# A two-layer transformer kernel: the order of the mixing layer, with gating moved on GpSimd and normalisation in pairs of tiles

## The chip, the cores and the metric

The kernel runs on one core of one Trainium2 chip. The metric is the device time of one execution in microseconds, the median of several runs. A core has five engines that run their own instruction lists in order and meet only at semaphores: TensorE (PE), VectorE (DVE), ScalarE (ACT), GpSimd (POOL) and SyncE (SP, which here issues transfers).

## The reference

The input is x, 2048 tokens of 256 numbers. Two layers follow one another, each with an attention-like part and a mixture of experts, both gated and modulated. The change touches only the first part of the second layer, the mixing layer:

```python
h = _layernorm(x, axis=-1) * (1 + ca) + sa          # outer normalisation, modulated
x = x + ga * _L1_attn_ref(h, ...)                   # ga: a vector of 256
# _L1_attn_ref(X, ...), X of 2048 rows:
Xn = _layernorm(X, gamma, beta)                     # nested normalisation
Q, K, V = jnp.split(Xn @ W_in + b_in, 3, axis=-1)
K, V = _rotary(K, 128), _rotary(V, 128)
A = jnp.sum(_cos_sim(K) * _cos_sim(V), axis=-2)
Y = (0.5 * A + 0.5)[:, None, :] * Q
return Y @ W_out + b_out + X                        # X is h, so x also gets ga * h
```

In the kernel the token axis is one sequence of 2048, as the input has batch 1.

## The kernel before

The tokens lie as 16 tiles of 128 (`NT = 16`), handled in quarters of four (`TQ = 4`, `NC = 4`). The mixing layer is `phase_mix` (line 1614). Each engine has its own block in it, with the order of its steps written out by hand.

Step by step for a quarter q, with the code's names:

- `stats(q)` (VectorE, `ln_stats`, lines 73 to 83) takes mean and variance of x; `outer(q)` on GpSimd (`ln_rstd`, line 103) raises the variance to the power -1/2; `outer_bias(q)` (VectorE, line 124) makes the bias; `outer(q)` on ScalarE (`ln_normal`, line 132) writes the normalised rows into `k.h`; `modulate(q)` (VectorE, lines 141 and 142) multiplies and adds.
- The same follows for the nested normalisation, from `k.h` into `xn`: `nested_stats(q)`, `nested(q)` on GpSimd, `nested_bias(q)`, `nested(q)` on ScalarE.
- `turn(q)` on TensorE transposes `xn` (line 150) into two PSUM banks `tp`, and `turned(q)` on ScalarE (line 1882) copies them to `xnT` with gamma and beta.

And for each tile i:

- `keys_values(i)` (TensorE, lines 1956 and 1958): first values, then keys, each in one of two PSUM banks. Keys of tile i wait until VectorE has finished tile i - 2.
- `products(i)` (VectorE): copies the values to SBUF (line 1780), waits for the first of the two `squares(i)` (ScalarE, line 1894, which give the norms), and makes the two products (lines 1783 and 1786).
- `turn_products(i)` (GpSimd, line 1712) multiplies by the rotation.
- After four tiles `token_weights(q)` (GpSimd, lines 1718 and 1722) makes the weights, and `sum_products(q)` (TensorE, line 1968) sums the quarter into `pA`.

Behind the last tile TensorE transposes expert weights of the next part (`turn_weights`, line 902), VectorE makes `A_rows` (lines 1830 to 1839), TensorE and VectorE make `A`, `w_sc` (1844), `w_c` (1846) and `b_all` (1848), and then the residual loop adds, tile by tile, the product `xnT` by `w_c` (TensorE, line 2024, two PSUM banks) to `k.x` (VectorE, line 1857) and takes the statistics for the router. At the head of each quarter VectorE adds `b_all` (line 1854). This needs `add_gated(q)` of GpSimd (lines 1726 and 1729): `k.h` times the gate `ga`, added to `k.x`.

The orders that matter here:

- GpSimd: the powers, then the rotations of all 16 tiles with `token_weights(q)` after each fourth, then `add_gated` of all four quarters.
- VectorE: `products(0)` to `products(3)` alternate with `nested_stats(2)`, `modulate(3)` and `nested_stats(3)`; `products(4)` to `products(15)` follow without normalisation between them.
- TensorE: `turn(q + 1)` stands behind `keys_values(4q + 1)`.
- ScalarE: ten weight copies (`keep_half`), `outer(0)` to `outer(2)`, two more copies, and later `nested(q + 2)` inside quarter q.
- SyncE: a weight load (`load_raw(4)`) waits for the last rotation; the weight transposes behind `A` need it.

## Time and profile before

| | |
|---|---|
| median of 3 runs | 1109.9 us (1108.56 to 1111.27) |
| the profiled execution, its own time | 1106.7 us |
| its span on the core | 1104.8 us, 24791 instructions |
| TensorE busy | 972.3 us (88%) |
| VectorE busy | 640.9 us (58%) |
| ScalarE busy | 521.5 us (47%) |
| GpSimd busy | 300.9 us (27%) |
| mixing layer | about 718 to 821 us of the span |

The profile shows one execution. A time in a row is the start in microseconds from the start of the span, followed by the duration. A bracket behind a row says how long the engine had been idle before it and who released it. The shares of the whole span say little on the mixing layer, which is a tenth of it: there the engines alternate, and the rows are read stage by stage.

### The profile page before, as it was taken

The numbers are of one execution on the slowest core, as the hardware profiler recorded it, in microseconds if no ns is written. First come the engines' busy times: TensorE is split into PE (matmuls) and PEld (weight loads), VectorE is DVE, ScalarE is ACT, GpSimd is POOL, SyncE is SP. The second block draws the span as 40 slices with busy tenths as digits, with TensorE's granted clock in tenths as the row PEclk, the third lists the DMA queues.
The fourth block names the chain that finished last, engine by engine and source line by source line (L and its number), as shares of the span: only waits on it lengthen the run. The fifth ranks groups of instructions, "written<-read, shape, count | busy, mean of one in ns | idle before, by whom it ended". The sixth has DMA issues, their size and how long they took to land. (4 is left out here: it accounts for less than half of the span.)

```text
span 1104.8 us, 24791 instructions
## 1 busy us (share of the span) xinstructions
PE 972.3 (88%) x9939; PEld 636.8 (58%) x9943; DVE 640.9 (58%) x1643; ACT 521.5 (47%) x813; POOL 300.9 (27%) x347
## 2 busy tenths in 40 slices
PE   7789899999999999886499999859857699999993
PEld 4334334445444444343277777647644699999993
DVE  5578999999799888754600000187586633333331
ACT  4434567777865875755121221276325233333330
POOL 2100510011011111230233432235830245554541
PEclk9888999999999999998699999969888799999997
DMA  5880000000000000007833785121324023222224
GB/s 187 181 170 4 2 2 3 2 3 3 2 3 2 3 3 3 3 2 251 261 113 102 203 251 166 20 77 58 119 66 141 24 46 50 47 47 48 47 43 96
DMA packets 63275, 78.81 MB, mean 71 GB/s; under 512 B 12096, under 2 KB 54976, under 8 KB 62736
## 3 DMA queue, kind: packets, MB, share of 16 engines
q1 hardware_dynamic: 50688, 61.54, 18.5%
q0 software_dynamic: 11968, 15.47, 8.8%
q8 instruction: 65, 1.06, 0.4%
q10 hardware_dynamic: 528, 0.52, 0.1%
q14 instruction: 26, 0.21, 0.1%
HBM read 58.12 MB, written 21.36 MB: 72 GB/s over the span
## 5 line engine op out<-in xcount | busy, mean ns | idle before, releaser
L594 ACT ACTIVATE k_prob<-f_s 128x1024 f32<-128x1024 f32 (+3 forms) x320 | 269.9, 896 | 119.2 <-PE f_s L432 118.6
L654 DVE TENSOR_REDUCE k_mpart<-f_r 128x1 f32<-128x512 f32 x384 | 250.6, 685 | 34.1 <-PE f_r L375 31.8
L375 PE MATMUL f_r<-k_ks,k_qs 112*32 112x512 bf16 (+3 forms) x2560 | 211.4, 356 | 19.6 <-DVE k_mpart L654 7.8
L432 PE MATMUL f_s<-k_qs,k_ks 114*32 114x512 bf16 (+3 forms) x2560 | 174.2, 349 | 1.9 <-ACT k_prob L594 1.3
L850 POOL TENSOR_SCALAR_AFFINE_SELECT k_prob<-k_prob 128x256 f32<-128x256 f32 x128 | 51.2, 406 | 380.8 <-ACT k_prob L594 379.6
L375 PEld LDWEIGHTS f_r<-k_ks,k_qs 112*32 112x32 bf16 x2560 | 70.0, 95 | 135.2 <-DVE k_mpart L654 55.9
L448 PE MATMUL f_o<-k_prob,k_vaug 128*32 128x512 f32 (+3 forms) x1280 | 146.0, 528 | 1.5 <-POOL k_prob L850 1.4
L651 DVE CUSTOM_DVE_ANT_0 k_unread<-f_r,k_causal 128x128 bf16<-128x128 f32 (+3 forms) x256 | 121.2, 484 | 17.2 <-PE f_r L375 16.0
L432 PEld LDWEIGHTS f_s<-k_qs,k_ks 114*32 114x32 bf16 x2560 | 65.5, 97 | 78.0 <-issue 27.1
L2192 DVE TENSOR_TENSOR mid<-silu_g,e_u 128x512 f32<-128x512 f32 x39 | 26.8, 688 | 111.3 <-PE e_u L2094 110.3
L1348 DVE SCALAR_TENSOR_TENSOR outr<-p_o,k_w,k_mod 128x256 f32<-128x256 f32 x16 | 7.7, 484 | 134.0 <-PE p_o L1283 134.0
L1319 ACT ACTIVATE mid<-p_h 128x320 f32<-128x320 f32 x64 | 28.0, 437 | 111.6 <-PE p_h L1272 111.6
L2094 PEld LDWEIGHTS e_g<-xT,k_rot_t 128*128 128x128 f32 x624 | 76.9, 195 | 4.5 <-ACT xT L2152 2.6
L2280 POOL DMA_INDIRECT sum<-y,k_row_of x39 | 62.1, 1593 | 63.7 <-DVE y L2203 52.7
L2094 PE MATMUL e_g<-xT,k_rot_t 128*128 128x128 f32 x624 | 77.6, 278 | 2.0 <-ACT xT L2152 2.0
L1272 PE MATMUL p_h<-rowsT,k_w1T 128*128 128x320 f32 x256 | 72.6, 442 | 6.5 <-issue 5.5
L2094 PE MATMUL e_u<-xT,k_rot_t 128*128 128x128 f32 x624 | 76.0, 275 | 0.0
L2105 PE MATMUL e_y<-k_w1T,mid 128*128 x312 | 73.6, 379 | 0.0
L2094 PEld LDWEIGHTS e_u<-xT,k_rot_t 128*128 128x128 f32 x624 | 72.8, 192 | 0.0
L912 POOL DMA_INDIRECT k_xb<-h_rows,k_tok_of x39 | 45.3, 1162 | 99.0 <-PE e_x L2088 53.5
L1272 PEld LDWEIGHTS p_h<-rowsT,k_w1T 128*128 128x128 f32 x256 | 48.9, 194 | 28.0 <-issue 9.5
L1366 POOL DMA_INDIRECT sum<-outr,k_row x24 | 37.8, 1576 | 98.1 <-DVE outr L1348 98.1
(388 smaller groups left out, 1288.3 us busy)
## 6 DMA issues: line engine op xcount, KB each, us to landing
k_w1T<-in_L_ffn_w_dram SPq DMA_DIRECT2D x18, 512.0 KB, 10.5
k_w1T<-in_L_ffn_wi_dram SPq DMA_DIRECT2D x8, 1024.0 KB
k_w1T<-in_L_ffn_wo_dram SPq DMA_DIRECT2D x8, 1024.0 KB
k_qs<-q_dram SPq DMA_DIRECT2D x6, 768.0 KB, 9.5
h_rows<-k_h SPq DMA_DIRECT2D x8, 512.0 KB, 4.8
sum<-k_x SPq DMA_DIRECT2D x8, 512.0 KB, 6.5
q_dram<-k_room SPq DMA_DIRECT2D x12, 256.0 KB, 9.3
k_rot_t<-in_L_ffn_w_dram SPq DMA_DIRECT2D x6, 512.0 KB, 4.8
```

The source lines that it names most:

```text
L375: last = nc.tensor.matmul(dst[32 * j:32 * (j + 1), :], qs[0:KROWS, c, GH * g + hs, q0:q0 + 32], ks[0:KROWS, QC * ck:QC * ck + w], start=Tr ...
L432: last = nc.tensor.matmul(sc[h % 2][32 * j:32 * (j + 1), i, off:QC], ks[0:KALL, k0:k0 + 32], qs[0:KALL, c, GH * g + 2 * pair + i, off:QC], ...
L448: last = nc.tensor.matmul(ot[32 * j:32 * (j + 1), off:QC], vaug[:, kt, :], prob[:, u % 2, j, off:QC], start=(kt == 0), stop=(kt == TQ * (c ...
L594: nc.scalar.activation(prob[:, u % 2, 2 * pair:2 * pair + 2, off:QC], sc[h % 2][:, :, off:QC], ACT.Exp, scale=HD ** -0.5).then_inc(e_done, 1)
L651: nc.vector.tensor_tensor_reduce(unread[:, r % RING, 0:w], bank(r)[:, 0:w], causal[:, QC - w:QC], 1.0, NEG, ALU.add, ALU.max, mpart[:, s % ...
L654: nc.vector.reduce_max(mpart[:, s % 2, hs, t, ck:ck + 1], bank(r)[:, 0:w], AX.X).then_inc(ring_used[r % RING], 1)
L850: nc.gpsimd.affine_select(out=block_, in_=block_, compare_op=ALU.is_ge, fill=0.0, base=0, pattern=[[0, 2], [1, P]], channel_multiplier=-1) ...
L912: nc.gpsimd.indirect_dma_start(out=k.xb[:, b % 2, :], out_offset=None, in_=k.h_rows, in_offset=bass.IndirectOffsetOnAxis(ap=k.tok_of[:, b: ...
L1272: last = nc.tensor.matmul(ph[n % 2][:, 0:CAP], wi[:, s, t, P * n:P * (n + 1)], rowsT[:, s, t, :], start=(t == 0), stop=(t == KH - 1))
L2094: last = nc.tensor.matmul(out[:, P * c:P * (c + 1)], w[:, s, F1 * t + P * c:F1 * t + P * (c + 1)], xT[:, s, t, :], start=(t == 0), stop=(t ...
L2105: last = nc.tensor.matmul(py[s][:, :], m[:, s, P * c:P * (c + 1)], k.w1T[:, e, 2, D * c:D * (c + 1)], start=(c == 0), stop=(c == FT - 1))
L2280: nc.gpsimd.indirect_dma_start(out=k.sum1, out_offset=bass.IndirectOffsetOnAxis(ap=k.row_of[:, b:b + 1], axis=0), in_=y[:, s, :], in_offse ...
```

## The change

Nothing is computed otherwise. The quarter is replaced by six spans in the two normalisations and the transposes: four pairs (tiles 0 and 1, 2 and 3, 4 and 5, 6 and 7) and two quarters (8 to 11, 12 to 15). The steps `span_stats`, `span_rstd`, `span_bias` and `span_normal` are the old ones over a span. A pair's four transposes go to one PSUM bank (`tp[g % 2]`) and are copied by two ScalarE instructions of 256 columns.

GpSimd's `add_gated(0)` to `add_gated(2)` stand between its rotations. The gating of the last quarter goes to VectorE, behind `products(15)`. Three of the four additions of `b_all` go from VectorE to GpSimd (`add_bias`). All engines get new orders:

```diff
+SPANS = [(0, 2), (2, 4), (4, 6), (6, 8), (8, 12), (12, 16)]
+PAIRED = 4
...
@@ block.gpsimd
             outer(0)
             outer(1)
             outer(2)
             nested(0)
+            nested(1)
             outer(3)
-            nested(1)
+            nested(2)
             pool.wait_ge(weights_in, 16 * MIX_LOADS)
             pool.wait_ge(tok_zero, 1)
+            outer(4)
             turn_products(0)
-            nested(2)
-            turn_products(1)
-            turn_products(2)
             nested(3)
-            for i in range(3, NT):
+            for i in range(1, 5):
                 turn_products(i)
-                if i % TQ == TQ - 1:
-                    token_weights(i // TQ)
-            for q in range(NC):
-                add_gated(q)
-            for q in range(NC):
+            token_weights(0)
+            add_gated(0)
+            nested(4)
+            outer(5)
+            for i in range(5, 10):
+                turn_products(i)
+            token_weights(1)
+            nested(5)
+            add_gated(1)
+            turn_products(10)
+            turn_products(11)
+            token_weights(2)
+            add_gated(2)
+            for i in range(12, NT):
+                turn_products(i)
+            token_weights(3)
+
+            def add_bias(q):
+                if q == NC - 1:
+                    pool.wait_ge(last_gated, 1)
+                nc.gpsimd.tensor_tensor(quarter(k.x, q), quarter(k.x, q), bcast(b_all[:, :], TQ),
+                                        ALU.add).then_inc(sum_ready, 1)
+
+            pool.wait_ge(wc_ready, 2)
+            for q in range(1, NC - 1):
+                add_bias(q)
+            ln_rstd(nc, pool, k, 0, var3_ready, rstd3_ready)
+            add_bias(NC - 1)
+            for q in range(1, NC):
                 ln_rstd(nc, pool, k, q, var3_ready, rstd3_ready)
...
@@ block.vector
             modulate(0)
             outer_bias(2)
             nested_stats(0)
-            stats(3)
+            modulate(1)
             nested_bias(0)
-            modulate(1)
-            outer_bias(3)
             nested_stats(1)
             modulate(2)
             nested_bias(1)
+            stats(3)
+            nested_stats(2)
+            outer_bias(3)
             products(0)
-            nested_stats(2)
+            nested_bias(2)
             products(1)
+            stats(4)
             modulate(3)
-            nested_bias(2)
+            nested_stats(3)
             products(2)
-            nested_stats(3)
+            nested_bias(3)
             products(3)
-            nested_bias(3)
-            for i in range(TQ, NT):
+            outer_bias(4)
+            products(4)
+            modulate(4)
+            products(5)
+            nested_stats(4)
+            stats(5)
+            nested_bias(4)
+            products(6)
+            outer_bias(5)
+            products(7)
+            products(8)
+            modulate(5)
+            products(9)
+            nested_stats(5)
+            nested_bias(5)
+            products(10)
+            products(11)
...
+            for i in range(12, NT):
                 products(i)
...
+            last = NC - 1
+            dve.wait_ge(normal_h, len(SPANS))
+            step(tt(quarter(k.h, last), quarter(k.h, last), bcast(gate, TQ), ALU.mult))
+            tt(quarter(k.x, last), quarter(k.x, last), quarter(k.h, last), ALU.add).then_inc(last_gated, 1)
             dve.wait_ge(A_done, 1)
...
                 if i % TQ == 0:
                     q = i // TQ
-                    dve.wait_ge(hb_ready, q + 1)
-                    tt(quarter(k.x, q), quarter(k.x, q), bcast(b_all[:, :], TQ), ALU.add).then_inc(sum_ready, 1)
-                    dve.wait_ge(sum_ready, q + 1)
+                    if q == 0:
+                        dve.wait_ge(hb_ready, 1)
+                        step(tt(quarter(k.x, 0), quarter(k.x, 0), bcast(b_all[:, :], TQ), ALU.add))
+                    else:
+                        dve.wait_ge(sum_ready, q)
...
@@ block.scalar
-            for n in range(IN_TAIL, AT_START - 2):
+            for n in range(IN_TAIL, 20):
                 keep_half(n)
             outer(0)
             outer(1)
             outer(2)
...
+            squares(3)
+            turned(3)
+            outer(4)
+            squares(4)
+            squares(5)
+            nested(4)
+            squares(6)
+            turned(4)
+            squares(7)
+            outer(5)
+            squares(8)
+            squares(9)
+            nested(5)
+            squares(10)
+            turned(5)
+            squares(11)
...
@@ block.tensor
-            for q in range(NC):
-                keys_values(TQ * q)
-                keys_values(TQ * q + 1)
-                if q + 1 < NC:
-                    turn(q + 1)
-                keys_values(TQ * q + 2)
-                if q >= 2:
-                    sum_products(q - 2)
-                keys_values(TQ * q + 3)
+            turns = {0: 1, 2: 2, 4: 3, 6: 4, 9: 5}
+            for i in range(NT):
+                keys_values(i)
+                if i in turns:
+                    turn(turns[i])
+                if i in (10, 14):
+                    sum_products(i // TQ - 2)
             sum_products(NC - 2)
             sum_products(NC - 1).then_inc(A_done, 1)
```

ScalarE's order ahead of `squares(3)`, left out above, is: `outer(0)` to `outer(2)`, `keep_half(20)`, `keep_half(21)`, `nested(0)`, `keep_half(22)`, `keep_half(23)`, `turned(0)`, `nested(1)`, `turned(1)`, `squares(0)`, `outer(3)`, `nested(2)`, `squares(1)`, `turned(2)`, `squares(2)`, `nested(3)`. In the names of the new orders the number of a normalisation, turn or bias step is that of a span, and the number of a product, square or rotation that of a tile.

## Rows read from the trace of the kernel before

**Rows 1.** Two stages: length, then each engine's busy time (instructions), granted clock.

```profile
737.00:757.00 20.00, 17.07 (x77) 13.20 (x78) 17.02 (x50) 13.64 (x37) 8.81 (x9) 0.80 0.00 0
757.00:782.00 25.00, 24.57 (x141) 17.53 (x139) 12.89 (x38) 14.36 (x54) 13.15 (x18) 1.00 0.21 64
```

**Rows 2.** Timeline of PE: start, duration, line, output and inputs, idle before.

```profile
737.69 1.94 PE L150 MATMUL m_tp<-k_ident,k_w1T 128*128 128x128 f32 x8 [10.08 <-ACT k_w1T L132]
740.58 0.37 PE L1956 MATMUL m_v<-m_b_part,m_share 128*128 128x256 bf16 x1 [0.96 <-ACT m_xnT L1882]
...
779.43 0.27 PE L1956 MATMUL m_k<-m_b_part,m_share 128*128 128x256 bf16 x1
...
784.58 1.06 PE L1968 MATMUL m_pA<-k_w1T,m_w_tok 128*32 128x512 f32 x8 [3.02 <-issue]
...
788.65 1.44 PE L902 MATMUL m_v<-k_ident,k_w1T 128*128 128x128 f32 x8
791.70 0.60 PE L2002 MATMUL m_tp<-m_ones,m_A_rows 128*128 128x1 f32 x4 [1.61 <-DVE m_A_rows L1839]
```

**Rows 3.** Timelines of PE, ACT and DVE: one tile's keys, square and product.

```profile
776.38 0.27 PE L1956 MATMUL m_k<-m_b_part,m_share 128*128 128x256 bf16 x1
...
777.55 0.38 ACT L1894 ACTIVATE m_sq<-m_k 128x256 f32<-128x256 f32 x1 [1.08 <-PE m_k L1958]
...
778.13 0.42 DVE L1783 TENSOR_TENSOR k_w1T<-m_k,m_vals 128x256 f32<-128x256 f32 x1 [0.99 <-ACT m_sq L1894]
```

**Rows 4.** Timelines of DVE, POOL and ACT: the steps of a quarter's normalisations.

```profile
721.92 1.41 DVE L77 BATCH_NORM_STATS2 k_stats<-k_x 128x6 f32<-128x256 f32 x4 [0.95 <-DMA k_x<-sum]
...
723.86 1.40 DVE L77 BATCH_NORM_STATS2 k_stats<-k_x 128x6 f32<-128x256 f32 x4
...
739.79 1.22 DVE L141 TENSOR_TENSOR k_h<-k_h,k_mod 128x1024 f32<-128x1024 f32 x1
...
742.18 0.16 DVE L124 SCALAR_TENSOR_TENSOR m_nbias<-m_mv,m_rstd 128x4 f32<-128x4 f32 x1
...
747.83 1.01 POOL L103 TENSOR_TENSOR m_rstd<-m_var,k_mhalf 128x4 f32<-128x4 f32 x1 [1.11 <-DVE m_var L82]
...
782.56 1.64 POOL L1718 TENSOR_TENSOR m_inv_n<-m_norm,k_mhalf 128x8 f32<-128x8 f32 x1
...
726.79 4.15 ACT L132 ACTIVATE k_h<-k_x,k_nbias,k_rstd 128x256 f32<-128x256 f32 x8
...
758.13 1.43 ACT L1882 ACTIVATE m_xnT<-m_tp,k_beta,k_gamma 128x512 f32<-128x512 f32 x2
```

**Rows 5.** Timelines of DVE and POOL, where both are at work.

```profile
786.36 0.22 DVE L1833 TENSOR_TENSOR m_A_sum<-m_A_sum,m_pA 128x64 f32<-128x64 f32 x1
...
786.87 2.38 POOL L1729 TENSOR_TENSOR k_x<-k_x,k_h 128x1024 f32<-128x1024 f32 x1
787.08 2.26 DVE L1838 TENSOR_TENSOR m_A_rows<-m_A_sum,m_A_dif 128x64 f32<-128x64 f32 x1
...
748.81 1.64 POOL L1712 TENSOR_TENSOR k_w1T<-k_w1T,k_rot_t 128x256 f32<-128x256 f32 x1
...
802.15 2.35 POOL L1729 TENSOR_TENSOR k_x<-k_x,k_h 128x1024 f32<-128x1024 f32 x1
802.87 0.42 DVE L1857 TENSOR_TENSOR k_x<-k_x,m_k 128x256 f32<-128x256 f32 x1
```

**Rows 6.** Line 884 between 780 and 785 us: the load's issue and its landing.

```profile
L884 SPq DMA_DIRECT2D k_rot_t<-in_L_ffn_w_dram x1: 507/507/507, 783.6 to 783.6; - x1
...
DMA to landing us min/median/max: 5.7/5.7/5.7
```

**Rows 7.** Timeline of PE: first and last matmuls of the residual loop.

```profile
799.22 5.34 PE L2024 MATMUL m_k<-m_w_c,m_xnT 128*128 128x256 f32 x24
...
817.05 1.13 PE L2024 MATMUL m_k<-m_w_c,m_xnT 128*128 128x256 f32 x4
```

**Rows 8.** A stage as in the first group, that follows the 3.02 us of idle PE.

```profile
786.00:789.00 3.00, 3.00 (x17) 3.00 (x15) 2.90 (x6) 1.87 (x4) 2.92 (x2) 0.51 1.07 371
```

More of the change, by code:

```diff
@@ L1611, in _, with span_of, span_stats, span_rstd @@
             gather_row1(nc, k, 0)
+SPANS = [(0, 2), (2, 4), (4, 6), (6, 8), (8, 12), (12, 16)]
+PAIRED = 4
+def span_of(i):
+    return next(g for g, (lo, hi) in enumerate(SPANS) if lo <= i < hi)
+def span_stats(nc, step, k, g, var_ready):
+    tiles = range(*SPANS[g])
+    for i in tiles:
+        last = nc.vector.bn_stats(k.stats[:, i, :], k.x[:, i, :])
+    step(last)
+    for i in tiles:
+        last = nc.vector.bn_aggr(k.mv[:, i, :], k.stats[:, i, :])
+    step(last)
+    s = slice(*SPANS[g])
+    nc.vector.tensor_scalar_add(k.var[:, s], k.mv[:, s, 1], EPS).then_inc(var_ready, 1)
+def span_rstd(nc, pool, k, g, var_ready, rstd_ready):
+    pool.wait_ge(var_ready, g + 1)
+    s = slice(*SPANS[g])
+    nc.gpsimd.tensor_tensor(k.rstd[:, s], k.var[:, s], k.mhalf[:, s], ALU.pow).then_inc(rstd_ready, 1)
+def span_bias(nc, dve, k, g, rstd_ready, bias_ready):
+    dve.wait_ge(rstd_ready, g + 1)
+    s = slice(*SPANS[g])
+    nc.vector.scalar_tensor_tensor(k.nbias[:, s], k.mv[:, s, 0], -1.0, k.rstd[:, s],
+                                   ALU.mult, ALU.mult).then_inc(bias_ready, 1)
+def span_normal(nc, act, k, g, bias_ready, norm_ready):
+    act.wait_ge(bias_ready, g + 1)
+    for i in range(*SPANS[g]):
+        last = nc.scalar.activation(k.h[:, i, :], k.x[:, i, :], ACT.Identity, bias=k.nbias[:, i:i + 1],
+                                    scale=k.rstd[:, i:i + 1])
+    last.then_inc(norm_ready, 1)
 def phase_mix(nc, k, a, sem):
@@ L1904, in _ @@
             outer(2)
-            for n in range(AT_START - 2, AT_START):
-                keep_half(n)
+            keep_half(20)
+            keep_half(21)
             nested(0)
+            keep_half(22)
+            keep_half(23)
             turned(0)
+            nested(1)
+            turned(1)
+            squares(0)
             outer(3)
-            nested(1)
-            for q in range(NC):
-                squares(TQ * q)
-                squares(TQ * q + 1)
-                if q + 1 < NC:
-                    turned(q + 1)
-                squares(TQ * q + 2)
-                if q + 2 < NC:
-                    nested(q + 2)
-                squares(TQ * q + 3)
+            nested(2)
+            squares(1)
+            turned(2)
+            squares(2)
+            nested(3)
+            squares(3)
[14 more added lines that the diff above has]
+            squares(11)
+            squares(12)
+            squares(13)
+            squares(14)
+            squares(15)
             for n in range(AT_START, IN_SUMS):
```

69 lines of the change are left out of this document (42 added, 27 removed).

## The prediction

> **What bounds the kernel now.** I read the stage table first, then the engines' timelines of the mixing layer. No engine bounds this layer throughout [rows 1]. Until about 757 us VectorE is the busy one (17.0 of 20 us); from there to 782 TensorE is busy 24.6 of 25 us. Each is held only where the orders of the engines meet, so I follow those. The reader is to see four places [rows 2]. TensorE waits 10.1 us for the first normalised quarter; `keys_values(0)` starts at 740.6. The last `sum_products` starts at 784.58, after the waits behind the last tile (its `k` product starts at 779.43, [rows 2]). `A_rows` comes only at 791.64, and PE had been free since 790.1. One tile at full clock is a `v` and a `k` product of 0.98 each; from the start of `k` to the square on ScalarE it is 1.17, to VectorE's product 1.75 [rows 3].
>
> **Prices of the parts** [rows 4]. A quarter's statistics take VectorE 1.94 (721.92 to 723.86, the next one's start), its modulation 2.39 (739.79 to 742.18), its normalisation on ScalarE 1.97 (eight tiles in 4.15, 0.49 each), `turned` 1.43. The power on GpSimd takes 1.01 for 4 columns and 1.64 for 8. No pair is in this trace. Estimates from halves plus the fixed part: statistics 1.15 (0.97 to 1.3), modulation 1.35 (1.2 to 1.5), normalisation 1.1, power 0.7 (0.5 to 1.0), `turned` 0.8 to 0.95. `products(i)` holds VectorE 1.0.
>
> **Earlier start.** ScalarE does eight weight copies ahead of `outer(0)`, no longer ten, so is free at 725.5, not 726.8. Then: normalisation 726.55, `modulate(0)` 727.9, nested statistics 729.2, power (it finds `modulate(1)` on VectorE and waits) 730.5, `nested(0)` 731.85, four transposes at half clock 732.95, `turned(0)` 733.9. `keys_values(0)` starts at 734.0: 6.6 us earlier than 740.6.
>
> **What the new orders do to that.** Here the in-order queues decide. Before, the later three quarters are normalised well ahead of PE's turns, which is why PE is busy 24.6 of 25 us there [rows 1]. After, four links are tight.
> - Tiles 0 to 3: `squares(0)` stands behind `turned(1)`, so behind PE's `turn(1)`; `products(0)` ends at 740.6, `products(1)` at 743.3. `products(2)` stands behind `stats(4)` 1.94, `modulate(3)` 1.35, `nested_stats(3)` 1.15; with its own copy (0.45) that is 748.3. `keys_values(4)` needs that copy and PE is free at 744.9: 3.5 us idle. `nested(3)` then lets `turn(3)` start at 750.5 (750.0 to 751).
> - `turn(3)` to `turn(4)`: transposes and signal 0.85, `turned(3)` 0.8, `outer(4)` 1.95, first half of `squares(4)` 0.6, end of `products(4)` 0.55, `modulate(4)` 2.4, `products(5)` 1.0, `nested_stats(4)` 1.95, `stats(5)` 1.95, bias 0.15, `nested(4)` 2.1: 14.3. To it come 0.7, the rotation of tile 4 that takes the port between the two modulation instructions (as in [rows 5] at 748.81), and 1.6, because GpSimd's `nested(4)` now stands behind `token_weights(0)` (1.9) and `add_gated(0)` (4.7) and its power is ready at 765.1 where VectorE is at 763.6. Sum 16.6 (14.1 to 17.5), so `turn(4)` is at 767.1. PE's own work in it (a turn, two tiles, some half clock) is 5 to 6 us. The rest is idle.
> - `turn(4)` to `turn(5)`: `turn(4)` 0.87 to 1.75, `v` of tile 7 0.98 to 1.9, `k` to ScalarE 1.17, `squares(7)` 0.8, `outer(5)` 1.95, first half of `squares(8)` 0.6, end of `products(8)` 0.55, `modulate(5)` with its port wait 3.1, `products(9)` 1.0, `nested_stats(5)` 2.05, GpSimd's power 1.0 behind `turn_products(9)` and `token_weights(1)` (0.65), bias 0.15, `nested(5)` 2.1: 16.2 to 18.7; with the clock half at first, I take 18.2: 785.3. PE waits in it after `keys_values(9)`, about 10 us.
> - `turn(5)` to the `k` of tile 15: 0.87, five tiles 9.75, one `v` 0.98, two `sum_products` 1.94 = 13.5 (to 15.5 at half clock first). I take 15.0: 800.3.
> So the last `k` starts 20.9 us later than 779.43. Lower bound 750.0 + 14.1 + 15.6 + 13.5 = 793.2 (+13.8), upper 751 + 17.5 + 19 + 15.5 = 803 (+23.6).
>
> **Behind the last tile.** Before, `sum_products(3)` starts 5.15 after that `k`. GpSimd now has `add_gated(2)` (4.7) just ahead of the last four rotations, and VectorE has its two gating instructions (1.2 each, two SBUF operands) in the same microseconds as the last rotation and power: they take turns at the port. I count 8.2 (6.2 to 8.5): +3.0 (+1.0 to +3.3).
>
> **What is gained.** GpSimd gates nothing while `A` is made. The first of the two 64-column instructions took 2.26, to the end of GpSimd's addition (786.87 + 2.38), where such a one takes 0.22 (the port again, [rows 5]); the second went the same way, and PE got `A_rows` at 791.7. It will be ready 4.3 us earlier. But PE is then late: it has weight transposes until 790.1, so only the 1.61 counts that PE waited [rows 2] (0.6 if they all run at half clock). The first `w_sc` instruction loses its port wait too, which hides behind PE's next three weight transposes. The weight load that these need was issued at 783.6, behind GpSimd's last rotation, and landed after 5.7, at 789.3 [rows 6]; it moves with that rotation, and PE asks 14 us after the last `k`, the load is there 13 us after it: hidden by 1 us. The residual loop runs on PE from 799.22 to 818.18, 19.0 us [rows 7]; PE waits in it for VectorE, which has a bias addition for each quarter. With three of the four on GpSimd (2.36 each, ready before their tiles: 802.2 and 804.6 on the old axis) it is PE's own 16 x 0.87 + 0.2 = 14.1, less 0.3 for the quarters' ends: a gain of 4.6 (3.3 to 5.1; the low end if `sum_ready` is late once).
>
> **Sum.** +20.9 + 3.0 - 1.6 - 4.6 = **+17.7 us**; bounds +13.8 + 1.0 - 1.6 - 5.1 = +8.1 and +23.6 + 3.3 - 0.6 - 3.3 = +23.0. The profiled execution took 1106.7 (span 1104.8, 1.9 around it), 3.2 below the median. Made against it the sum gives 1124.4; the median moves alike, 1109.9 + 17.7 = 1127.6, and goes on record. Bounds 1118 and 1133.
>
> **Two places where rows and the skill meet.** While GpSimd's gating ran (802.15, 2.35) VectorE's addition with one PSUM operand took 0.42 as ever, while one with two SBUF operands waited to GpSimd's end [rows 5]. The Trainium skill (SBUF — State Buffer, "SBUF: two separate sides") has the same: an exclusive lock, only for a VectorE instruction with two SBUF inputs or in a two-port mode. By the rows `products` runs freely beside `add_gated`; were it locked too, six gating instructions of 2.4 could each hold one up, 14 us more.
> After 3.02 us with PE idle [rows 2] the granted clock is 0.51 from 786 to 789, the 1.2 GHz level [rows 8]. The Trainium skill (TensorE: Matmul & The Clock Gate, "HAM oscillation — how this bites in real kernels") warns that idle gaps between bursts bring the slow clock back each time. It speaks against this change: every one of its waits restarts slow. By the rows one restart costs about 1.5 us (3 us at half rate); all three together are 4.5 of my +20.9.
>
> **The rivals.**
> - The bare order (20%). The links hold, but the soft terms don't: no port waits, `add_gated(0)` over before anyone asks, the clock up again at once. That is the lower bound with some slack, 1113 to 1120, likeliest 1118. For it: pair prices are estimates and ScalarE has room. Against it: GpSimd's order has 6.6 us fixed ahead of `nested(4)`.
> - Faster (9%): the early start is kept. If VectorE's work interleaved without waits, PE would run 38 us from 734 and end about 7 us earlier: -6.6 + 3.0 - 1.6 - 4.6 = -9.8, 1100. For it: VectorE's work of the layer (45 us) fits under PE's. It decides where `nested(4)` ends before `keys_values(6)`, at about 757. Against: VectorE alone, without one wait, has by the prices above 29.5 us of steps ahead of that bias, 721.9 + 29.5 = 751.4, and my walk puts 12 us of waits into them.
> - The parts cancel (4%): 1108 to 1112.
> - Worse than forecast (9%), the other way: gating's 2.4 us holds also small VectorE steps (variance, bias), or GpSimd wins the port against the first bias addition and delays the residual loop by 2.4. 1133 to 1138.
> - Forecast 58%: 1120 to 1133.
>
> **How the numbers follow.** The range 1113 to 1133 holds the forecast and the bare order, 0.78, and the rest of it a little. A measurement of this kernel can tell about 0.2% (2.2 us) from no change. Faster 0.09, same 0.04, slower 0.87. Cases of one sign hold most of it.
>
> **What would show it.** In the profile after: first `keys_values` near 734; then PE idle of 3 to 4 us before tile 4, of some 10 us before `turn(4)` and again before `turn(5)`, both released by ScalarE's normalisation; granted clock near 0.5 behind each; the last `sum_products` 22 to 25 us later; the two `A_rows` instructions at 0.22; residual quarters of 3.5 us. The forecast is wrong if `turn(4)` or `turn(5)` start without a long wait, or if GpSimd's powers never stand behind gating.

## The result, and the profile after

The changed kernel takes **1128.6 us** (median of 4 runs, 1128.32 to 1128.77), the kernel before beside it 1109.6 (4 runs, 1108.56 to 1111.27): a ratio of 1.0162, with a 95% interval of 1.0146 to 1.0178. It is 19.0 us slower; 17.7 had been forecast, 1127.6 in 1113 to 1133. The profiled execution of after took 1128.6 (span 1126.7), that of before 1106.7 (span 1104.8). So the two traces differ by 21.9 us and the medians by 19.0, because the profiled execution of before lay 2.9 below its median.

Where the 21.9 us lie is read by cutting both traces at the same two instructions: the first PE transpose of the mixing layer's `w_in`, and the first transpose of the router behind it. The layer takes 108.73 us before and 130.26 after, 21.53 more. The time ahead of the layer is 1.48 shorter, the time behind it 1.85 longer, and the change touches neither. In the profiled executions of the twelve kernels the layer starts between 716.7 and 722.5 us, and what follows it takes 276.9 to 279.9. The median of the kernel before was taken four times beside the others and lay between 1108.7 and 1111.6. So a difference of a few microseconds between two medians may have nothing to do with an edit inside the layer. I compare whole kernels by their ratios and edits by the length of the layer and its steps. These lengths come from one profiled execution of each kernel. How well they repeat is seen where an edit touches only what comes later: the last `k` stands at 87.23 in after and at 86.98 in `after_tail`. Where the clock differed by chance the difference is 1.7 us, as told at `norm_early`.

The page of after first, in 40 slices of 28.2 us: busy tenths of PE, then the granted clock.

```profile
span 1126.7 us, 24812 instructions
...
PE   7789999999999999968599999663777599999993
...
PEclk9989999999999999997799999886897799999997
```

The slice from 760.5 to 788.7 us has a 3 for PE and a 6 for the clock. That is the stretch where before PE was busy 24.6 of 25 us [rows 1]. The stage table of after (columns as in [rows 1]) has the same two stages, then four of 3 to 4 us: behind the waits for the fifth and sixth span, behind the last wait for token weights, and the `w_sc` products:

```profile
737.00:757.00 20.00, 15.13 (x71) 11.33 (x69) 10.78 (x35) 12.32 (x38) 6.11 (x7) 0.91 0.00 1
757.00:782.00 25.00, 8.38 (x38) 6.74 (x38) 16.18 (x46) 9.47 (x28) 14.95 (x13) 0.72 0.00 0
768.20:772.20 4.00, 4.00 (x17) 3.55 (x18) 1.12 (x4) 2.26 (x6) 0.73 (x1) 0.63 0.00 0
788.50:792.50 4.00, 3.96 (x17) 3.52 (x18) 0.35 (x1) 0.00 (x0) 0.28 (x1) 0.60 0.18 18
812.00:815.00 3.00, 2.94 (x13) 1.31 (x14) 0.92 (x5) 0.00 (x0) 0.00 (x0) 0.50 1.09 374
819.00:823.00 4.00, 4.00 (x27) 3.64 (x26) 1.71 (x3) 1.83 (x5) 0.55 (x1) 1.00 0.38 137
```

PE works 8.4 of 25 us, and no other engine is full there either (VectorE 16.2, GpSimd 15.0): a chain of steps across engines has taken over. PE's timeline shows where it is waited for; these rows answer to [rows 2] and [rows 7].

```profile
732.76 0.37 PE L2086 MATMUL m_v<-m_b_part,m_share 128*128 128x256 bf16 x1 [1.20 <-ACT m_xnT L1983]
...
747.26 0.37 PE L2086 MATMUL m_v<-m_b_part,m_share 128*128 128x256 bf16 x1 [3.42 <-DVE m_vals L1853]
...
750.89 0.60 PE L2075 MATMUL m_tp<-k_ident,k_w1T 128*128 128x128 f32 x4
...
768.20 1.97 PE L2075 MATMUL m_tp<-k_ident,k_w1T 128*128 128x128 f32 x8 [11.41 <-ACT k_w1T L1655]
...
788.54 1.97 PE L2075 MATMUL m_tp<-k_ident,k_w1T 128*128 128x128 f32 x8 [11.96 <-ACT k_w1T L1655]
...
803.90 0.27 PE L2086 MATMUL m_k<-m_b_part,m_share 128*128 128x256 bf16 x1
...
812.06 1.93 PE L2098 MATMUL m_pA<-k_w1T,m_w_tok 128*32 128x512 f32 x8 [6.02 <-issue]
...
817.45 0.50 PE L2130 MATMUL m_tp<-m_ones,m_A_rows 128*128 128x1 f32 x4
...
819.15 1.89 PE L2137 MATMUL m_tp<-m_w_sc,m_wqT 128*128 128x256 f32 x8
...
823.06 15.18 PE L2152 MATMUL m_k<-m_w_c,m_xnT 128*128 128x256 f32 x64
```

`keys_values(0)` starts at 732.76, tile 4 after 3.42 us of idle, `turn(4)` after 11.41, `turn(5)` after 11.96, the last `k` at 803.90, the last `sum_products` at 812.06. The table gives the steps of all kernels, described below, in microseconds from the layer's start, worked out from the timelines of PE. Columns with a plus count from the step before them. `turn(4)` and `turn(5)` are the turns of tiles 8 to 11 and 12 to 15. Y is the length of the residual's products, and the last column that of the whole layer.

| kernel | first keys | turn(4) | turn(5) | last k | sum_products(3) | A's product | Y starts | Y | layer |
|---|---|---|---|---|---|---|---|---|---|
| before | 22.43 | - | - | 61.28 | +5.15 | +7.12 | +7.52 | 18.96 | 108.73 |
| after | 16.09 | 51.53 | 71.87 | 87.23 | +8.16 | +5.39 | +5.61 | 15.18 | 130.26 |
| gate_only | 22.20 | - | - | 61.53 | +9.18 | +6.12 | +5.61 | 15.18 | 106.32 |
| pairs_only | 16.04 | 48.95 | 67.07 | 83.43 | +5.16 | +7.23 | +7.37 | 19.02 | 130.90 |
| turns_late | 16.53 | 52.19 | 72.21 | 85.27 | +7.06 | +5.81 | +5.61 | 15.19 | 127.64 |
| filled | 16.03 | 50.35 | 69.30 | 83.16 | +8.15 | +5.84 | +5.61 | 15.19 | 126.64 |
| powers_first | 16.08 | 48.57 | 67.50 | 85.01 | +8.71 | +6.00 | +5.61 | 15.18 | 129.20 |
| norm_early | 15.88 | 37.05 | 52.83 | 65.15 | +8.72 | +6.42 | +5.62 | 15.17 | 109.78 |
| early_tail | 15.07 | 37.98 | 53.76 | 66.05 | +5.15 | +4.94 | +5.87 | 15.18 | 105.88 |
| early_free | 16.03 | 39.51 | 55.11 | 69.99 | +5.15 | +5.32 | +5.73 | 15.18 | 110.07 |
| gate_tail | 22.28 | - | - | 61.29 | +5.15 | +5.21 | +5.84 | 15.18 | 101.36 |
| after_tail | 16.06 | 51.32 | 71.63 | 86.98 | +5.15 | +5.19 | +5.88 | 15.19 | 127.08 |

After against before: last `k` +25.95, `sum_products(3)` +3.01, `A`'s product -1.73, start of Y -1.91, Y itself -3.78. Sum +21.5, the layer's difference. (Between the end of Y and the router's transpose lie 8.7 us in every one of them.)

### The profile page after: what moved, and what is told of

Read it like the earlier page. It is cut to its first block and busy times, and to the rows that moved or that the text cites. A ratio compares the mean times of both kernels' runs of the same rounds, so it can differ in the third digit from the quotient of the medians.

```text
span 1126.7 us, 24812 instructions
## 1 busy us (share of the span) xinstructions
PE 974.5 (86%) x9939; PEld 638.9 (57%) x9943; DVE 640.4 (57%) x1654; ACT 521.7 (46%) x817; POOL 307.5 (27%) x352
## 5 line engine op out<-in xcount | busy, mean ns | idle before, releaser
L651 DVE CUSTOM_DVE_ANT_0 k_unread<-f_r,k_causal 128x128 bf16<-128x128 f32 (+3 forms) x256 | 121.1, 484 | 17.3 <-PE f_r L375 16.2
## 6 DMA issues: line engine op xcount, KB each, us to landing
k_w1T<-in_L_ffn_w_dram SPq DMA_DIRECT2D x18, 512.0 KB, 10.4
```

Source lines behind the costliest of these rows:

```text
L651: nc.vector.tensor_tensor_reduce(unread[:, r % RING, 0:w], bank(r)[:, 0:w], causal[:, QC - w:QC], 1.0, NEG, ALU.add, ALU.max, mpart[:, s % ...
```

## Experiments

The theory to be tested: the pairs' orders put the steps of spans 4 and 5 late in the in-order queues of VectorE, ScalarE and GpSimd, and PE waits for them; the moved gating pays in the tail and costs inside. ("The port" below is short for what [rows 5] show: a VectorE instruction with two operands in SBUF, the core's on-chip memory, and a GpSimd instruction wait for each other.) The rivals: the turns stand too early in PE's own order; the slow clock behind the waits is the cost; GpSimd's gating ahead of the powers is.

### Each half alone: gate_only and pairs_only

`gate_only` is the kernel before with the gating and the bias additions moved as in the change. `pairs_only` is the kernel after with both as they were.

```diff
gate_only, against before
             for i in range(3, NT):
                 ...
                     token_weights(i // TQ)
-            for q in range(NC):
-                add_gated(q)
+                    if i // TQ < NC - 1:
+                        add_gated(i // TQ)
 (with add_bias on GpSimd and the last gating on VectorE, as in the change)
pairs_only, against after
             token_weights(0)
-            add_gated(0)
             nested(4)
...
             nested(5)
-            add_gated(1)
...
             token_weights(2)
-            add_gated(2)
 (with four add_gated behind the last token_weights and four bias additions on VectorE, as before)
```

> The kernel before with only the gating half of the change: add_gated(0) to (2) each behind its token_weights on GpSimd, the last quarter gated on VectorE behind products(15), three of the four bias additions on GpSimd. Quarters and all orders of normalisation as before. If the order of the normalisations costs the time (my theory): GpSimd falls behind by the last rotations, sum_products(3) starts 8 to 9.5 us after the last k product where it was 5.15, so +3 to +4.3; A_rows -1.7, faster products behind it up to -1.9 (clock), residual loop -3.8: together -1 to -4, so 1106 to 1109. If the gating between the rotations is what costs (rival): well above before, 1120 or more, with most of the 19 us.

> The changed kernel with only the other half: spans, pairs and the new orders of normalisation stay; all four add_gated stand behind the last token_weights again, no gating on VectorE, all bias additions on VectorE. My theory: the long waits of TensorE ahead of turn(4) and turn(5) stay, each 1.5 to 2.3 us shorter because no gating stands before the power or holds the bias instruction; the last k product is 22 us later than before, nothing is gained behind it: 1129 to 1132. Rival (gating costs): close to before, 1110 or under.

Measured: `gate_only` 1108.0 us (10 runs, 1103.4 to 1109.3) against 1111.6, ratio 0.996 (0.9944 to 0.9976): faster by 0.4%, as expected, and its layer is 2.4 us shorter. `pairs_only` 1133.2 (1131.7 to 1133.8), ratio 1.0202 (1.0174 to 1.023), where 1129 to 1132 was expected; layer +22.2. **The whole loss comes with the pairs and their orders**: last `k` +22.15 by them alone. What the gating does is a loss and a gain that nearly cancel. With the pairs it costs 3.8 us up to the last `k` (87.23 against 83.43); behind the last tile it costs 3.0 (4.0 in `gate_only`), then gives back 1.8 + 1.8 + 3.8 (1.0 + 1.9 + 3.8 in `gate_only`). In `gate_only`, where nothing is late inside, the last `k` moves by 0.25 only.

### Where the turns stand: turns_late

```diff
-            turns = {0: 1, 2: 2, 4: 3, 6: 4, 9: 5}
+            turns = {0: 1, 2: 2, 4: 3, 7: 4, 11: 5}
```

> The changed kernel with one line different: turn(4) stands behind keys_values(7) and turn(5) behind keys_values(11), so TensorE has one and two tiles more to do while it waits. Theory (the start of turn(4) and turn(5) is set by the chain over VectorE, GpSimd and ScalarE and not by TensorE): both turns start nearly when they did (within 1 us), and the work behind them shrinks by one and two tiles: 5 to 7 us faster than the changed kernel, 1122 to 1124. Rival (TensorE's own work or its clock sets the pace): under 1 us of gain, 1128.

Measured: 1127.7 us (1124.0 to 1129.8), ratio 1.0144 (1.0108 to 1.018); layer -2.6 where 5 to 7 were expected, and the time outside the expected 1122 to 1124. The starts of the two turns do not move (+0.66 and +0.34), so the chain and not PE's order sets them: that part of the theory held. The gain beyond them I had sized wrong. The last `k` follows `turn(5)` after 13.06 us instead of 15.36, 2.3 less and not the 3.9 of two tiles:

```profile
770.73 1.97 PE L2075 MATMUL m_tp<-k_ident,k_w1T 128*128 128x128 f32 x8 [5.90 <-ACT k_w1T L1655]
773.57 0.40 PE L2086 MATMUL m_v<-m_b_part,m_share 128*128 128x256 bf16 x1 [0.87 <-ACT m_xnT L1983]
773.76 1.91 PE L2088 MATMUL m_v<-k_w_in,m_xnT 128*128 128x256 f32 x4
```

The tiles that used to follow the turn are done before it, so PE waits for `turned` itself, and the next `v` comes while the clock is still down (1.91, where the same product takes 1.03 at full clock).

### What the slow clock costs: filled

PE transposes its identity into a scratch bank while it waits; no engine reads that bank.

```diff
             turns = {0: 1, 2: 2, 4: 3, 6: 4, 9: 5}
+            extra = {3: 7, 6: 24, 9: 26}
+            pe.wait_ge(k.w_act, AT_START - BY_DVE0)
             for i in range(NT):
                 keys_values(i)
+                for _n in range(4 * extra.get(i, 0)):
+                    nc.tensor.transpose(pw[:, 0:P], k.ident[:, :], k.ident[:, :])
```

The added `wait_ge` is there because the bank first serves for weight transposes, which ScalarE must have copied.

> The changed kernel with transposes of the identity into an unused PSUM bank on TensorE, 28, 96 and 104 of them, in its three long waits (ahead of keys_values(4), turn(4), turn(5)), so that it does not idle there. If the slow clock behind each wait costs about 1.5 us each, as I worked out: the granted clock stays at 1.0 in the stretches behind, and the time is 3.5 to 5 us shorter, 1124 to 1125. If the clock costs nothing here because other engines set the pace there: within 1 us of 1128.6.

Measured: 1127.9 us (1126.1 to 1129.1), ratio 1.0147 (1.0118 to 1.0176); the last `k` comes 4.07 earlier, the layer is 3.6 shorter. The layer is as expected; the whole kernel is only 0.7 below after and misses the expected 1124 to 1125. In its profiled execution the layer starts 5.0 later than in that of after. PE behind the wait, and the stage behind it:

```profile
772.01 1.09 PE L2075 MATMUL m_tp<-k_ident,k_w1T 128*128 128x128 f32 x8 [0.98 <-ACT k_w1T L1655]
...
772.00:776.00 4.00, 3.99 (x25) 3.40 (x26) 1.45 (x5) 3.06 (x11) 0.73 (x1) 1.00 0.00 0
```

Eight transposes in 1.09 us instead of 1.97, clock 1.00 instead of 0.63. In the layer the slow clock costs 4 us for the three waits: with it gone, 22 of the 26 us are still there.

### Whether the steps are late: norm_early

After, with the same pairs and the same gating, but statistics, modulation, normalisation and powers of spans 4 and 5 ahead of the products that they stood behind (VectorE's order below; ScalarE's follows it, on GpSimd `nested(4)` and `nested(5)` stand ahead of `add_gated(0)` and `add_gated(1)`, and the last turn stands after tile 10):

```diff
             outer_bias(3)
+            stats(4)
             products(0)
             nested_bias(2)
+            outer_bias(4)
             products(1)
-            stats(4)
             modulate(3)
...
             nested_bias(3)
-            products(3)
-            outer_bias(4)
-            products(4)
             modulate(4)
-            products(5)
+            products(3)
             nested_stats(4)
-            stats(5)
+            products(4)
             nested_bias(4)
-            products(6)
+            stats(5)
+            products(5)
             outer_bias(5)
-            products(7)
-            products(8)
+            products(6)
             modulate(5)
-            products(9)
+            products(7)
             nested_stats(5)
+            products(8)
             nested_bias(5)
+            products(9)
```

> The changed kernel with the same parts, spans and gating, but the steps of spans 4 and 5 earlier in the orders: stats(4) ahead of products(0), modulate(4) and nested_stats(4) about two tiles earlier, modulate(5) and nested_stats(5) behind products(6) and (7), ScalarE, GpSimd and TensorE to match (turn(5) behind keys_values(10)). My theory (the 26 us are the lateness of these steps): TensorE waits under 3 us ahead of turn(4) and turn(5), the last k product starts 58 to 66 us into the layer (87.2 in the changed kernel, 61.3 before), the rest as in the changed kernel: 1102 to 1110. Rival (two normalisations in pairs cost it by themselves, through more instructions and more meetings of the engines): over 1120.

Measured: 1109.5 us (8 runs, 1108.1 to 1112.8) against 1110.8, ratio 0.9992 (0.9975 to 1.001). The last `k` comes at 65.15 instead of 87.23 us. **Of the 26 us, 22.1 are gone with the order of those steps**, with the pairs and all of the moved gating left in. (The slow clock behind the waits, 4 us by `filled`, is in them: it goes with the waits.) This is the deciding run: `turn(4)` starts after 1.39 us of idle and `turn(5)` after 0.86, both at full clock.

```profile
737.83 1.03 PE L2091 MATMUL m_v<-k_w_in,m_xnT 128*128 128x256 f32 x4
...
758.89 1.09 PE L2078 MATMUL m_tp<-k_ident,k_w1T 128*128 128x128 f32 x8 [1.39 <-ACT k_w1T L1655]
...
764.24 0.28 PE L2089 MATMUL m_v<-m_b_part,m_share 128*128 128x256 bf16 x1 [2.31 <-ACT m_xnT L1986]
...
768.78 0.27 PE L2089 MATMUL m_v<-m_b_part,m_share 128*128 128x256 bf16 x1 [2.41 <-DVE m_vals L1856]
...
774.67 1.09 PE L2078 MATMUL m_tp<-k_ident,k_w1T 128*128 128x128 f32 x8 [0.86 <-ACT k_w1T L1655]
```

Some of the 22.1 is luck of this execution. Its first `v` takes 1.03 us, at full clock, where that of after, `early_tail` and `early_free` takes 1.91. `early_tail` has the same orders up to its last rotations. Counted from the first keys, its `turn(4)` comes at 22.91 us and its last `k` at 50.98; here they come at 21.17 and 49.27. So 1.7 us belong to the clock at the start, and the order is worth about 20. The whole kernels say the same: +19.0 us for after, -1.3 here.

But the first keys start 6.55 us earlier than before and the last `k` 3.87 later, so 10.4 us of the early start are lost inside, 12 without that luck. Two things speak for what takes them. Most of PE's remaining waits (2.41 above, and others of 0.8 to 1.9) end on VectorE's `m_vals`. And the pairs do not save VectorE work. Ahead of the first keys it is busy 13.4 us instead of 20.0; between first keys and last `k` it is busy 37.5 instead of 25.4. So 6.5 us of its work have moved behind the first keys, and 5.6 have been added, waits at the port included: in `pairs_only`, without the moved gating, the added part is 2.2. That this is the cause was not isolated.

### GpSimd's powers ahead of the gating: powers_first

```diff
-            token_weights(0)
-            add_gated(0)
             nested(4)
             outer(5)
+            token_weights(0)
+            add_gated(0)
             for i in range(5, 10):
                 turn_products(i)
-            token_weights(1)
             nested(5)
-            add_gated(1)
+            token_weights(1)
             turn_products(10)
+            add_gated(1)
             turn_products(11)
```

> The changed kernel with GpSimd's order alone different in two places: nested(4) and outer(5) ahead of token_weights(0) and add_gated(0), nested(5) ahead of token_weights(1), and add_gated(1) behind turn_products(10), so that the power never waits for gating and VectorE's bias instruction of span 5 doesn't find a gating instruction on the port. If this is the difference of pairs_only to the changed kernel (turn(4) 2.6 and turn(5) 4.8 us earlier there), the last k product starts 3.5 to 4.8 us earlier than in the changed kernel: 1124 to 1125.5. If the difference came from somewhere else (for example the load of GpSimd as a whole): under 1 us.

Measured: 1128.9 us (1125.6 to 1131.1), ratio 1.0148 (1.012 to 1.0176), a miss: 1124 to 1125.5 was expected. `turn(4)` comes 2.96 earlier and `turn(5)` 4.37, close to what was expected; the last `k` only 2.2, where 3.5 to 4.8 was expected, and the layer 1.1. The rest went where GpSimd's `add_gated(1)` went:

```profile
796.76 2.36 POOL L1772 TENSOR_TENSOR k_h<-k_h,k_mod 128x1024 f32<-128x1024 f32 x1
...
799.59 2.57 DVE L1913 TENSOR_TENSOR k_b_out<-k_b_out,k_mod 128x256 f32<-128x256 f32 x1
```

VectorE's small product of `b_out` (0.95 in after) now takes 2.57, beside the gating's second instruction, with the products of the last tiles queued behind it, and PE waits 1.66 us for one of them. Much of the gating's price has moved, not gone.

### Gating behind the last token weights: gate_tail, early_tail, after_tail, early_free

In all four, `add_gated(2)` stands behind `token_weights(3)`, and VectorE's gating of the last quarter behind `A_rows`, its addition behind the first `w_sc`. `gate_tail` has it on `gate_only` (whose inner `add_gated` are then two), `early_tail` on `norm_early`, `after_tail` on after. `early_free` has it on `norm_early` too; in addition `add_gated(0)` stands behind `nested(5)`, and `add_gated(1)`, which stood there already, two rotations later.

```diff
             token_weights(2)
-            add_gated(2)
             for i in range(12, NT):
                 turn_products(i)
             token_weights(3)
+            add_gated(2)
+            pool.wait_ge(hb_ready, 3)
             pool.wait_ge(wc_ready, 2)
...
             tt(out[:, :, 1], A_sum[:, :], A_dif[:, :], ALU.subtract).then_inc(Arow_ready, 1)
+            dve.wait_ge(normal_h, len(SPANS))
+            step(tt(quarter(k.h, last), quarter(k.h, last), bcast(gate, TQ), ALU.mult))
...
+            tt(quarter(k.x, last), quarter(k.x, last), quarter(k.h, last), ALU.add).then_inc(last_gated, 1)
             dve.wait_ge(wc_done, 1)
early_free, further against norm_early
-            add_gated(0)
             turn_products(5)
...
             nested(5)
+            add_gated(0)
             token_weights(1)
+            turn_products(8)
+            turn_products(9)
             add_gated(1)
```

> The kernel before with the gating half, as in gate_only, but GpSimd's add_gated(2) behind its last token_weights and VectorE's two gating instructions of the last quarter behind A_rows and w_sc. gate_only lost 4.0 us between the last k product and sum_products(3) (9.18 against 5.15). If that was gating ahead of the last rotations: sum_products(3) at 5.2 again, the rest as in gate_only, the layer 102 to 103.5 us long (108.7 before), 1103 to 1105.5. Rival: add_gated(2) now holds A_rows at the port by more than TensorE's own 5.5 us, and half or more of the gain goes: 1106 to 1108.

> norm_early and the end of gate_tail together. If the two are independent: 2.5 to 3 us less than norm_early, and of all kernels the fastest, 1099 to 1107. If not (gate_tail's gating runs into something else with pairs): no better than gate_tail.

> The changed kernel with only the end of gate_tail: add_gated(2) behind the last token_weights, the last quarter's gating behind A_rows and w_sc. The last k product stays where it is (87.2 us into the layer), sum_products(3) starts 5.2 us behind it and not 8.16, the rest within 0.5: the layer is 3 us shorter, 1125 to 1126.5. If gating ahead of the last rotations wasn't the cause: no change, 1128.6.

> early_tail with add_gated(0) behind GpSimd's nested(5) in place of ahead of it. In norm_early the modulation of span 5 took 1.92 and 3.25 us beside add_gated(0), where it takes 1.22 each, and turn(4) to turn(5) was 15.8 us. If that is the port, modulate(5) is back at 2.4 to 3.1, turn(5) comes 2 to 3 us earlier and the last k product starts at 63 to 64.5 us into the layer: 1102 to 1103.5. It stays behind gate_tail (61.3, 1100.7) if VectorE, which has no free time in the first 38 us, is what eats the earlier start of keys_values(0); if it were the port alone, it would be ahead: under 1100.

Measured:
- **`gate_tail` 1100.7 us** (1098.4 to 1102.6) against 1110.8, ratio **0.9901** (0.9877 to 0.9924): faster than both kernels, and than the expected 1103 to 1105.5. Its layer takes 101.36, 7.4 less than before: last `k` and `sum_products(3)` as before, `A` -1.9, start of Y -1.7, Y -3.8.
- `early_tail` 1105.1 (1104.4 to 1105.2), ratio 0.994 (0.9923 to 0.9957): its layer is 3.9 shorter than that of `norm_early`, a little more than the expected 2.5 to 3. Of it 3.6 lie in `sum_products(3)`. I had expected it to be the fastest of all, and it is not: without the pairs the last `k` comes 4.8 earlier than with them, even well ordered.
- `after_tail` 1130.2 (1129.2 to 1131.3) against 1108.7, ratio 1.0183 (1.0148 to 1.0219). `sum_products(3)` is back at +5.15 and the layer 3.2 shorter, as expected, but the whole kernel is no faster: in its profiled execution the layer starts 4.7 later than in that of after. That an edit of 3 us in the layer shows in the time stays unconfirmed here.
- `early_free` 1112.5 (10 runs, 1107.4 to 1113.5) against 1108.7, ratio 1.0013 (0.9993 to 1.0034): a miss. I had expected the last `k` at 63 to 64.5; it came at 69.99, later than in `norm_early` and `early_tail`.

What `early_free` did, in the timelines of GpSimd and VectorE:

```profile
772.33 2.36 POOL L1772 TENSOR_TENSOR k_h<-k_h,k_mod 128x1024 f32<-128x1024 f32 x1
...
772.39 2.31 DVE L1647 SCALAR_TENSOR_TENSOR m_nbias<-m_mv,m_rstd 128x4 f32<-128x4 f32 x1
```

`modulate(5)` takes 2.8 us, as planned. The gating instead sits right behind `nested(5)`'s power, where its first instruction holds the bias step that the same power released. That is one part of the miss: from `turn(4)` to `turn(5)` there are 15.60 us, against 15.78 in `norm_early`, where 2 to 3 less were expected. A second part lies behind `turn(5)`, from which the last `k` is 14.88 away instead of 12.32. PE had waited 2.62 us, its clock was down (the turn took 1.97, the sum behind it 1.73), and it then waited 1.27 for VectorE, whose product for `w_out`, 0.68 in after, took 1.94 beside `add_gated(1)`. The rest, 2.3 us between first keys and `turn(4)`, is for the most part that run's lucky clock at the start.

The tail in `gate_tail`, in the timelines of GpSimd, VectorE and PE, to be held against [rows 2], [rows 5] and [rows 7]:

```profile
785.05 2.35 POOL L1726 TENSOR_TENSOR k_h<-k_h,k_mod 128x1024 f32<-128x1024 f32 x1
787.48 2.36 POOL L1729 TENSOR_TENSOR k_x<-k_x,k_h 128x1024 f32<-128x1024 f32 x1
...
788.30 1.63 DVE L1850 TENSOR_TENSOR m_A_dif<-m_A_mix 128x64 f32<-128x64 f32 x1
789.96 0.23 DVE L1852 TENSOR_TENSOR m_A_rows<-m_A_sum,m_A_dif 128x64 f32<-128x64 f32 x1
...
785.20 1.93 PE L1988 MATMUL m_pA<-k_w1T,m_w_tok 128*32 128x512 f32 x8 [3.02 <-issue]
...
790.41 0.57 PE L2022 MATMUL m_tp<-m_ones,m_A_rows 128*128 128x1 f32 x4
...
796.25 15.18 PE L2044 MATMUL m_k<-m_w_c,m_xnT 128*128 128x256 f32 x64
```

One `add_gated` lies beside the making of `A`, where before all four follow one another. It still holds one small VectorE instruction for 1.63 us, but ends at 789.8, and PE has weight transposes to do until 790.4: it no longer waits.

## Why the prediction was right, and where its steps were off

Times of after in this section are put on the axis of before: each is 1.48 us more than in the rows of after.

- **The mechanism.** The forecast said that the early start is given back twice over at two links between in-order queues, with some 10 us of idle PE ahead of `turn(4)` and again ahead of `turn(5)`, both released by ScalarE's normalisation. PE waited 11.41 and 11.96, released as said, and `norm_early` shows that the order of those steps is worth 20 to 22 us, clock included. GpSimd's powers ahead of the gating, alone, make 2.2 of it (`powers_first`).
- **First keys** 734.24, forecast 734.0. **Idle ahead of tile 4** 3.42, forecast 3.5. **`turn(3)`** 752.37, forecast 750.5 (750 to 751): 1.9 late. The first step that was off: I had put tile 4 at full clock, and behind 3.42 us of idle its `v` took 1.92 and its `k` 1.70. (I had counted three restarts of the clock in the sum, but in the walk up to `turn(3)` there is none. In `filled`, without it, `turn(3)` comes 1.29 earlier.)
- **`turn(3)` to `turn(4)`** 17.31, forecast 16.6 (14.1 to 17.5). `add_gated(0)` stands ahead of `nested(4)`'s power as said (762.52 + 2.34, then the power). What I had not counted is how GpSimd got there: the power of `token_weights(0)` took 2.61 beside VectorE's modulation. Two variance steps of 0.17 took 1.34 and 0.67 beside the gating, but VectorE then still waited 0.98 for the power, so they cost nothing here.
- **`turn(4)` to `turn(5)`** 20.34, forecast 18.2 (to 18.7; 19 in the upper bound). This is the term that was mis-sized most. Timelines of GpSimd and VectorE of after, then VectorE of `pairs_only`, whose times are within 0.03 us of those of after here:

```profile
783.04 1.01 POOL L1640 TENSOR_TENSOR m_rstd<-m_var,k_mhalf 128x4 f32<-128x4 f32 x1
784.02 2.34 POOL L1772 TENSOR_TENSOR k_h<-k_h,k_mod 128x1024 f32<-128x1024 f32 x1
...
784.09 2.29 DVE L1647 SCALAR_TENSOR_TENSOR m_nbias<-m_mv,m_rstd 128x4 f32<-128x4 f32 x1 [1.74 <-POOL m_rstd L1640]
```

```profile
784.12 0.16 DVE L1647 SCALAR_TENSOR_TENSOR m_nbias<-m_mv,m_rstd 128x4 f32<-128x4 f32 x1 [1.74 <-POOL m_rstd L1640]
```

  The bias step of `nested(5)` is 128 x 4. With `add_gated(1)` next in GpSimd's queue it takes 2.29 us, without it 0.16. PE waits for just this. I had the mechanism among the rivals, as the small VectorE steps that gating holds, at 9%. It belonged into the sum: the order puts `add_gated(1)` directly behind the power that releases the bias, so the collision is not a matter of chance.
- **The two links without gating.** In `pairs_only` they take 14.86 and 18.12 us. My walk, less the 1.6 for gating in the first, had 15.0 and 18.2. So the steps were priced right, and what failed was the price of gating: 1.6 in all, where after against `pairs_only` shows 2.45 and 2.22.
- **`turn(5)` to the last `k`** 15.36, forecast 15.0. **Last `k`** therefore +25.95, forecast +20.9, and above my upper bound of +23.6. The bound failed at the start of `turn(3)` and at the second link, as above: 1.4 and 1.3 us past their ends.
- **The clock.** I put 1.5 us on each restart, 4.5 in all; `filled` measured 4.07 at the last `k`. After 11.41 us of idle the eight transposes took 1.97 against 1.09, at a granted clock of 0.63 over 4 us, which is a first part at 1.2 GHz and a rest at 2.4. The Trainium skill (TensorE: Matmul & The Clock Gate, "HAM oscillation — how this bites in real kernels") names such gaps as what brings the slow clock back. The trace of after agrees, with 0.63 and 0.60 behind the two. It was a part of the loss and not its cause.
- **Behind the last tile** `sum_products(3)` 8.16 us after the last `k`, forecast 8.2: +3.01 for +3.0. `add_gated(2)` ends at 805.4, then the four rotations take 4.74 beside VectorE's two gating instructions at 1.63 each. In all three `*_tail` kernels and `early_free`, with `add_gated(2)` and VectorE's gating both moved, it is 5.15 again; which of the two does it was not separated.
- **`A`'s product** -1.73, forecast -1.6: `A_rows` in 0.23 and 0.22, and PE no longer waits. **Start of Y** -1.91, forecast 0. Here I left a term out. Before, PE idles 1.61 us for `A_rows` [rows 2]; in after it does not, and has the clock at 1.00 through the `w_sc` products. Eight of these take 1.89 in after and 3.01 before, so most of the 1.91 is the clock. `pairs_only`, with the gating of before, has +7.37 for this step.
- **Y** -3.78, forecast -4.6 (3.3 to 5.1). It takes 15.17 to 15.19 in all kernels with three bias additions on GpSimd, against the 14.1 that I made of 16 x 0.87. A quarter takes 3.8 us at a clock of 1.00, not the 3.5 that I had named as a sign; what adds the rest was not looked into.
- **A sign that did not come true.** The last `sum_products` was to start 22 to 25 us later. It starts 28.96 later (25.95 + 3.01).

So the sum was +20.9 + 3.0 - 1.6 - 4.6 = +17.7, and the traces have +25.95 + 3.01 - 1.73 - 1.91 - 3.78 = +21.5. The time came out 1.0 us from the forecast partly by luck, because errors cancelled. The last `k` came 5.1 us later than forecast and Y gained 0.8 less. Against that the start of Y gained 1.9 that were not forecast, and the medians moved by 2.9 us less than the two traces, as told above. The sign, the places and the tail were right; the inner links were sized with too little for the gating at the port.

Of the rivals, the faster one held that the early start is kept. `norm_early`, in which the steps are early and the gating is that of after, doesn't keep it: ratio 0.9992, while `gate_only`, with quarters and the same gating, has 0.996. That VectorE's work, which now comes behind the first keys, eats the early start is argued from its busy time and not shown. The bare order fails by the restarts of the clock and the price of gating, both measured above.

## What to carry to other kernels

In a pipeline of in-order queues an earlier first tile gains nothing by itself: look for the step that is needed last, several tiles on, and at what it stands behind in each queue. Put a long GpSimd instruction on two SBUF operands where VectorE has nothing small that PE waits for; directly behind a power whose result VectorE turns into a bias was the worst place here (2.29 and 2.31 us for a step of 0.16). If a change has two parts, measure each alone: here one part was worth having, and better still with its last piece moved behind the last result that anyone waits for.

## What the runs showed of the hardware

- The port is waited for by the smallest instructions. A 128 x 4 scalar-tensor-tensor of 0.16 us took 2.29 in after and 2.31 in `early_free`; a 128 x 4 tensor-scalar of 0.17 took 1.34 in after, to the end of the first gating instruction beside it. The Trainium skill (SBUF — State Buffer, "SBUF: two separate sides") has an exclusive lock for VectorE instructions with two SBUF inputs or in a two-port mode. The bias step has two such inputs; its 2.29, nearly the whole 2.34 of GpSimd's instruction, agrees. The variance step has one; in which mode it ran no run shows.
- GpSimd gets in between two instructions of a VectorE sequence, and VectorE between two of GpSimd's:

```profile
755.50 1.22 DVE L1841 TENSOR_TENSOR k_h<-k_h,k_mod 128x1024 f32<-128x1024 f32 x1
756.75 1.63 DVE L1842 TENSOR_TENSOR k_h<-k_h,k_mod 128x1024 f32<-128x1024 f32 x1
...
755.66 1.63 POOL L1758 TENSOR_TENSOR k_w1T<-k_w1T,k_rot_t 128x256 f32<-128x256 f32 x1 [4.38 <-DVE k_w1T L1859]
757.26 2.61 POOL L1764 TENSOR_TENSOR m_inv_n<-m_norm,k_mhalf 128x8 f32<-128x8 f32 x1
```

  In these rows of after the rotation of one tile, 0.73 alone, waits for the first modulation and ends at 757.29. The second modulation takes 1.63 where alone it is 1.22, and the power that follows takes 2.61 instead of 1.63. The order of the engines at the port is read from these times: no record shows it directly.
- Before, the clock fell again a little behind the wait of 1.61 us for `A_rows` [rows 2], which had followed one of 3.02. A stage of before, with the `w_sc` products in it:

```profile
793.30:796.30 3.00, 3.00 (x10) 2.36 (x9) 0.84 (x1) 1.37 (x3) 3.00 (x2) 0.50 0.00 0
```

  PE is busy for all 3 us at 0.50, and the eight products took 3.01 us against 1.89. In after the clock is 0.50 behind the 6.02 us wait at 812, yet 1.00 through the stage from 819, with no wait between. In `gate_tail` PE waits the same 3.02 us and then no second time; its clock is 1.00 from 791 to 794, and from `A`'s product to the start of Y it takes 5.84 instead of 7.52. So the shorter of two close waits cost more than its length, 1.61 of wait and 1.7 behind it.
- The clock behind the same waits can come out either way. In `norm_early` and `early_free` the last waits of PE ahead of the first keys are 3.4, 0.25 and 1.20 us, in the same order of steps. From 737.8 to 741.8 the granted clock is 1.00 in the one and 0.50 in the other. Between `norm_early` and `early_tail` the like difference was worth 1.7 us up to the last `k`.
- The time of the rest of the kernel is not fixed. The layer's start moved by 5.8 us, and the length of what follows the layer by 3.0, between profiled executions of kernels that are the same there.
